# Quartered Grams, moved MLP steps and full-float first lookups in a DLRM tower on one core

## The reference

```
e = stack([tbl_f[ids[:, f]] for f in range(26)], axis=1)      # 2048 x 26 x 128
combined = concatenate([e, dense_x[:, None, :]], axis=1)       # 2048 x 27 x 128
interact = einsum('bfd,bgd->bfg', combined, combined)          # one Gram per sample
z = interact[:, TRIU_I, TRIU_J]                                # 351 pairs
h = concatenate([z, dense_x], axis=1)                          # 2048 x 479
h = maximum(h @ W_top1 + b_top1, 0)                            # 512
h = maximum(h @ W_top2 + b_top2, 0)                            # 256
y = h @ W_top3                                                 # 1
```

## Time and profile before

| | us |
|---|---|
| median of 3 runs | 373.54 (372.81 to 373.73) |
| the profiled execution's own time | 373.32 |
| its span | 371.3 |
| TensorE busy | 340.5 (92%) |
| GpSimd busy (gather issue) | 260.9 (70%) |
| ScalarE busy | 184.3 (50%) |
| VectorE busy | 169.0 (46%) |

### The profile page before, as it was taken

How to read it: one execution, slowest core, us unless ns; L and a number is a source line. 1 busy time by engine, 2 the same in 40 slices (tenths; PEclk the granted TensorE clock), 3 DMA queues, 4 the chain that set the end, 5 groups by cost and what they waited for, 6 DMA issues and landing times.

```text
span 371.3 us, 13577 instructions
## 1 busy us (share of the span) xinstructions
PE 340.5 (92%) x6176; PEld 314.7 (85%) x6176; DVE 169.0 (46%) x380; ACT 184.3 (50%) x233; POOL 260.9 (70%) x265
## 2 busy tenths in 40 slices
PE   0698498889998999999999999999999999999997
PEld 0698497778988988999899998999888989998887
DVE  1999156533533535356244535356244635350220
ACT  3697222583436543473717643473726734375433
POOL 6688777777777777777777777777777777776000
PEclk9999799999998999999999999999999999999999
DMA  7984723212532226221252225321262222222000
GB/s 258 393 307 121 240 60 136 66 51 52 133 128 72 51 51 172 90 69 49 61 201 53 66 52 159 100 67 51 57 209 54 64 53 65 53 56 56 16 4 4
DMA packets 15773, 37.14 MB, mean 100 GB/s; under 512 B 5125, under 2 KB 7813, under 8 KB 15716
## 3 DMA queue, kind: packets, MB, share of 16 engines
q0 software_dynamic: 8192, 16.79, 17.8%
q1 hardware_dynamic: 7524, 19.48, 15.1%
HBM read 36.24 MB, written 0.01 MB: 98 GB/s over the span
## 4 chain that ended last, share of the span: by engine, by line
PE 68%; POOL 20%; issue 7%; DMA 2%; ACT 1%; DVE 1%; SPq 0%; ACTq 0%
PE ps_lk L465 30%; POOL rows L229 20%; PE ps_gram L492 10%; PE ps_tr L477 6%; PE ps_zt L518 6%; PE ps_mlp L518 6%; PE ps_mlp L525 3%; PE ps_zt L525 3%; PE ps_mlp L533 2%; PE ps_lk L546 1%; PE ps_zt L505 1%; DMA ids<-in_ids_onehot 1%; DMA rows<-in_tbl,gather_ids 1%; DVE table L288 1%; PE ps_lk L553 0%
## 5 line engine op out<-in xcount | busy, mean ns | idle before, releaser
L229 POOL DMA_INDIRECT rows<-in_tbl,gather_ids x256 | 259.6, 1014 | 80.5 <-issue 77.1
L465 PE MATMUL ps_lk<-onehot,table 128*128 128x256 f32 x1280 | 167.7, 290 | 14.1 <-DVE onehot L264 13.6
L465 PEld LDWEIGHTS ps_lk<-onehot,table 128*128 128x128 f32 x1280 | 160.4, 197 | 15.3 <-issue 13.9
L264 DVE TENSOR_SCALAR onehot<-ids_from 128x512 fp32r<-128x512 f32 x320 | 125.5, 443 | 92.7 <-PE ps_lk L465 77.0
L332 ACT COPY xt<-ps_tr 128x512 f32<-128x512 f32 x64 | 77.1, 1205 | 93.4 <-PE ps_tr L477 93.4
L492 PEld LDWEIGHTS ps_gram<-xt 128*26 128x26 f32 x4096 | 44.3, 104 | 21.5 <-issue 20.0
L492 PE MATMUL ps_gram<-xt 128*26 128x26 f32 x4096 | 52.6, 193 | 7.6 <-issue 4.3
L322 ACT COPY xt<-ps_lk 128x512 f32<-128x512 f32 x40 | 48.8, 1234 | 17.6 <-PE ps_gram L492 9.0
L272 DVE STREAM_TRANSPOSE zs<-ps_gram 128x832 f32<-128x832 f32 x16 | 16.8, 1050 | 84.2 <-PE ps_gram L492 80.6
L477 PE MATMUL ps_tr<-ident,rows 128*128 128x128 f32 x256 | 39.6, 278 | 6.7 <-DMA rows<-in_tbl,gather_ids 6.1
L477 PEld LDWEIGHTS ps_tr<-ident,rows 128*128 128x128 f32 x256 | 30.1, 141 | 10.0 <-issue 6.4
(11 more groups left out here) (51 smaller groups left out, 128.1 us busy)
## 6 DMA issues: line engine op xcount, KB each, us to landing
ids<-in_ids_onehot SPq DMA_DIRECT2D x8, 768.0 KB
ids<-in_ids_onehot SPq DMA_DIRECT2D x8, 512.0 KB
rows<-in_tbl,gather_ids POOLq DMA_INDIRECT x256, 2.6
w<-in_tbl SPq DMA_DIRECT2D x6, 512.0 KB, 7.5
h<-in_tbl SPq DMA_DIRECT2D x2, 512.0 KB, 5.8
zt<-in_tbl SPq DMA_DIRECT2D x2, 512.0 KB, 6.4
dense_x<-in_dense SPq DMA_DIRECT2D x8, 128.0 KB
zt<-in_dense SPq DMA_DIRECT2D x8, 128.0 KB, 2.9
```

The source lines that it names most:

```text
L229: pool.indirect_dma_start(rows[n % ROW_BUFS][:, r, :], None, t_[f"tbl_{GATHERED[r]}"], bass.IndirectOffsetOnAxis(ap=gather_ids[:, n, r:r + ...
L264: nc.vector.tensor_scalar(onehot[:, u % RING, :, :], ids_from[:, 2 * i:2 * i + 2, :], float(k), None, ALU.is_equal).then_inc(s_unit, 1)
L465: m = nc.tensor.matmul(bank(c, i)[:, j, :], table[:, 2 * i + j, part, k, :], onehot[:, u % RING, j, :], start=(k == 0 and j == 0 and part ...
```

## The change

- **Grams in quarters.** `PARTS` goes from 2 to 4: a Gram call has 32 matmuls. Between two quarters mostly stands an MLP step or a few transposes. The first quarter of tile 0 now stands ahead of `layer1(c-1, 0)` where the half stood behind it, and the first quarter of tile 1 ahead of `layer2(c-1, 0)`.
- **Gathers in eights as before.** A constant `EIGHTS = 2` keeps the half tiles; the Gram counts waited for are doubled, and the start's table `LEAD` is (0, 2, 8, 14, 20) in place of (0, 2, 6, 10, 16).
- **First pair in full floats.** `lookup_first` takes tables 0 and 1 for chunk 0 from their raw buffers, 16 fp32 matmuls in place of 32 fp32r ones, and so needs no high and low parts. These are made last (`SPLIT`), for chunk 1.
- **Start.** The ids of the first two tables are loaded and shifted apart; a tiny activation ahead of them loads ScalarE's table early. Tables from 2 on share three buffers.
- **Order in chunks 0 and 1.** Some transposes and copies stand at other places.

```diff
-PARTS = 2
-LEAD = (0, 2, 6, 10, 16)
+PARTS = 4
+EIGHTS = 2
+LEAD = (0, 2, 8, 14, 20)
+SPLIT = list(range(2, NO)) + [0, 1]
...
-                        pool.wait_ge(s_gpart, max(b - 2 * PARTS, 0) + 1)
+                        pool.wait_ge(s_gpart, (max(b - 2 * EIGHTS, 0) + 1) * (PARTS // EIGHTS))
...
+            def lookup_first():
+                for k in range(KT):
+                    pe.wait_ge(s_unit, k + 1)
+                    for j in range(2):
+                        if k == 0:
+                            pe.wait_ge(s_raw[j], 16)
+                        m = nc.tensor.matmul(bank(0, 0)[:, j, :], raw[j][:, k, :], onehot[:, k, j, :].bitcast(F32),
+                                             start=(k == 0 and j == 0), stop=(k == KT - 1), skip_group_check=True)
+                    if k % USE == USE - 1:
+                        m.then_inc(s_unit_used, 1)
...
             act.wait_ge(s_first, 1)
-            shift_ids(0, 0)
-            for j in range(3):
-                high(j)
+            nc.scalar.activation(warm[:, :], first[:, :], ACT.Identity)
+            shift_first(0, 2, s_ids_a, s_from_a)
+            shift_first(2, CUT[1], s_ids[0], s_from)
+            for n in range(2):
+                high(n)
             shift_ids(0, 1)
...
                 lookup(c, 4)
...
+                gram(c, 0, 0)
                 layer1(c - 1, 0)
-                gram(c, 0, 0)
+                gram(c, 0, 1)
                 if c + 1 < CHUNKS:
                     lookup(c + 1, 0)
                 turn(c, 1, 0)
                 layer1(c - 1, 1)
                 turn(c, 1, 1)
+                gram(c, 0, 2)
                 layer1(c - 1, 2)
-                gram(c, 0, 1)
+                gram(c, 0, 3)
                 turn(c, 1, 2)
                 layer1(c - 1, 3)
                 turn(c, 1, 3)
                 if c + 1 < CHUNKS:
                     lookup(c + 1, 1)
+                gram(c, 1, 0)
                 layer2(c - 1, 0)
-                gram(c, 1, 0)
+                gram(c, 1, 1)
                 if c + 1 < CHUNKS:
                     turn(c + 1, 0, 0)
                     lookup(c + 1, 2)
                     turn(c + 1, 0, 1)
+                gram(c, 1, 2)
                 layer2(c - 1, 1)
                 if c + 1 < CHUNKS:
                     turn(c + 1, 0, 2)
-                gram(c, 1, 1)
+                gram(c, 1, 3)
```

More of the change, by code:

```diff
@@ L104, in build @@
         y = sb("y", [P, TILES])
-        raw = [b[:, a:a + n, :].rearrange("p a s -> p (a s)").rearrange("p (k d) -> p k d", k=KT)
-               for b, a, n in ((h1, 0, T1), (zt, 0, NZ + 1), (w1, 0, 2), (w1, 2, 2), (w2, 0, T1))]
-        RAWS = len(raw)
+        stage = [b[:, a:a + n, :].rearrange("p a s -> p (a s)").rearrange("p (k d) -> p k d", k=KT)
+                 for b, a, n in ((h1, 0, T1), (zt, 0, NZ + 1), (w1, 0, 2), (w1, 2, 2), (w2, 0, T1))]
+        RAWS = len(stage) - 2
+        raw = [stage[j] if j < 2 else stage[2 + (j - 2) % RAWS] for j in range(NO)]
         ps_lk = [pb(f"ps_lk{i}", [P, 2, CS]) for i in range(LB)]
@@ L191, in load_raw @@
             def load_raw(j):
-                if j >= RAWS:
-                    sp.wait_ge(s_low, j - RAWS + 1)
-                sp.dma_start(raw[j % RAWS][:, :, :], t_[f"tbl_{ONE_HOT[j]}"].rearrange("(p k) d -> p k d", k=KT)
+                if j >= 2 + RAWS:
+                    sp.wait_ge(s_low, j - RAWS - 2 + 1)
+                sp.dma_start(raw[j][:, :, :], t_[f"tbl_{ONE_HOT[j]}"].rearrange("(p k) d -> p k d", k=KT)
                              ).then_inc(s_raw[j], 16)
             sp.dma_start(gather_ids[:, :, :], t_["ids_gather"].rearrange("p (t f) -> p t f", t=TILES)).then_inc(s_gids, 16)
-            load_ids(0, 0)
-            for j in range(3):
+            load_first_ids()
+            for j in range(4):
                 load_raw(j)
             load_ids(0, 1)
-            for j in range(3, NO):
+            for j in range(4, NO):
                 load_raw(j)
@@ L285, in _, with low @@
             nc.vector.tensor_copy(first[:, :], first_i[:, :]).then_inc(s_first, 1)
-            for j in range(NO):
-                dve.wait_ge(s_high, j + 1)
-                nc.vector.tensor_tensor(table[:, j, 1, :, :], raw[j % RAWS][:, :, :],
+            def low(n):
+                j = SPLIT[n]
+                dve.wait_ge(s_high, n + 1)
+                nc.vector.tensor_tensor(table[:, j, 1, :, :], raw[j][:, :, :],
                                         table[:, j, 0, :, :].bitcast(F32), ALU.subtract).then_inc(s_low, 1)
-                if j % 2 == 1:
-                    make_units(0, (j - 1) // 2 * KT, (j + 1) // 2 * KT)
+            make_units(0, 0, KT)
+            for i in range(1, LP):
+                low(2 * i - 2)
+                low(2 * i - 1)
+                make_units(0, i * KT, (i + 1) * KT)
+            low(NO - 2)
+            low(NO - 1)
             dve.wait_ge(s_const, 3)
@@ L308, in _, with high, shift_first @@
         def _(act):
-            def high(j):
+            def high(n):
+                j = SPLIT[n]
                 act.wait_ge(s_raw[j], 16)
-                nc.scalar.copy(table[:, j, 0, :, :], raw[j % RAWS][:, :, :]).then_inc(s_high, 1)
+                nc.scalar.copy(table[:, j, 0, :, :], raw[j][:, :, :]).then_inc(s_high, 1)
+            def shift_first(a, b, ready, done):
+                act.wait_ge(ready, 16)
+                nc.scalar.activation(ids_from[:, a:b, :], ids[0][:, a:b, :], ACT.Identity,
+                                     bias=first[:, :]).then_inc(done, 1)
             def shift_ids(c, h):
@@ L566, in _ @@
             pe.wait_ge(s_ident, 2)
-            for i in range(LP):
+            lookup_first()
+            turn(0, 0, 0)
+            for i in range(1, LP):
                 lookup(0, i)
-                turn(0, i // NGR, i % NGR)
+                if i < NGR:
+                    turn(0, 0, i)
             gram(0, 0, 0)
+            gram(0, 0, 1)
             lookup(1, 0)
-            gram(0, 0, 1)
+            gram(0, 0, 2)
+            turn(0, 1, 0)
+            gram(0, 0, 3)
             turn(0, 1, 1)
@@ L577, in _ @@
             turn(0, 1, 3)
-            gram(0, 1, 0)
-            gram(0, 1, 1)
+            for q in range(PARTS):
+                gram(0, 1, q)
             for c in range(1, CHUNKS):
```

41 lines of the change are left out of this document (25 added, 16 removed).

## The result

| | before | changed | 
|---|---|---|
| median, us | 373.18 (4 runs, 372.41 to 373.73) | 383.06 (4 runs, 382.96 to 384.04) |
| the profiled execution, us | 373.32 | 384.04 |
| its span, us | 371.3 | 381.9 |

The ratio is 1.0261, with a 95% interval of 1.0224 to 1.0297: 9.9 us slower. The profiled execution of the changed kernel is the slowest of its four, by 1 us; its span is 10.6 us longer than that of before.

The account below looks back on a forecast made before the run. Gathers were taken to bound the kernel up to 115 us, TensorE after it. Terms -1.65 + 9.4 + 0.8 - 2.0 + 0.5 = +7.05 us on 373.32 gave 380.4, with an 8-in-10 range of 375.5 to 387.

Parts of the forecast that it names:

- The new wait: First quarters behind lookup 4 and the last turn wait for ScalarE's copy: six stalls of 1.35 us and one of 1.3, +9.4.
- The start: Opening: first matmul at 8.8, eight matmuls done by 14.1, ninth gather at 14.65 in place of 16.30 us: -1.65 us.
- the step that earlier gathers give the same time back at the end: Up to 115 us gathers set the time, so starting the ninth 1.65 us earlier was counted in full as -1.65.
- TensorE's arrival: Chunk 2, turn 3: TensorE there at about 110 us, rows at 113.3, so gathers cover changes in its earlier waits.
- Cuts: Gram halves of chunks 2 to 7 cut into quarters: 0.08 us saved for each of 24 halves, -2.0, bounds -6 and +5.
- the quarter itself: A Gram quarter of 32 matmuls was put at 0.55 us plus 0.2 of edge, 0.75 in all.
- The small wait at the chunk's end: Chunk ends 2 to 6: PE reaches turn 3 some 0.15 us before the copy it needs; +0.8, bounds 0 and 2.
- The clock: TensorE's low clock after the row wait near 114 us stays and may last longer: +0.5, bounds 0 and 1.5.
- Rival 1: The new stalls also lower TensorE's clock, near 1.4 us each, six of them 8.4: 388.8 us; chance 0.10.
- Rival 2: Pauses and edges both vanish in Gram quarters, each cut half saving 0.5 us: -2.95, 370.4 us, faster; chance 0.07.
- Rival 3: Pauses come as often per matmul as before and each Gram cut adds 0.2: +4.8 for -2.0, 387.2 us; chance 0.09.
- Rival 4: No difference: pauses gone, edges stay (-6), earlier gathers in full, stalls at lower bound, no clock: +0.75, 374.1 us; chance 0.06.

Follow-up runs that it names:

- e1: The changed kernel with first Gram quarters put back behind layer 1 step 0 in chunks 2 to 7, and behind layer 2 in the last: 372.92 us, ratio 0.9978.
- e2: The kernel before, in halves, with the first half moved ahead of layer 1 in chunks 2 to 7 and ahead of layer 2 in the last: 383.58 us.
- e4: The change's start and order of chunk 0 alone, with Gram halves and the order of the kernel before from chunk 1 on: 374.20 us, ratio 1.0018.
- e7: The kernel before with only LEAD's second number 1 in place of 2, so the ninth gather may start earlier: 373.63 us, ratio 0.9998.
- e5: The changed kernel with turn 3 of tile 2 (chunk 1) behind layer 1 step 0 again, waits of chunks 2 to 7 kept: 382.20 us, ratio 1.025.
- e3: The kernel before with only the second half of each tile cut into quarters, an MLP step between, the first half in one piece: 374.65 us, ratio 1.002.
- e10: The kernel before without the gathers of tiles 6 to 15: 408.43 us on another chip, where before took 489.65, ratio 0.8414.
- e12: The kernel before with LEAD's second number 1 and VectorE's ten low-part subtractions replaced by multiplications by 0: 487.37 us on a chip where before took 489.65.

## Why the prediction was right

380.4 us were forecast with a range of 375.5 to 387, and 383.06 measured: +7.05 forecast, +9.9 found. The large term was right; the small ones were not, and two of their errors nearly cancel.

- **The new wait: right in mechanism, place and nearly in size.** +9.4 forecast, +10.6 by e1 and +9.9 by e2, from seven stalls of 1.26 to 1.30 us in the profile, 8.9 in all. From the start of lookup 4 to that of the Gram 5.33 us pass (209.21 to 214.54), where 3.92 passed to the next operation before: 1.41 a time against the 1.35 forecast. What goes beyond is 0.7 to 1 us that these two runs don't share out cleanly (e1 also takes away cuts, e2 has its pause and clock).
- **The start: the mechanism was wrong.** -1.65 was forecast; e4 measured between -0.1 and +1.5. Three steps failed. The second table landed later than I had read from the rows: the second matmul came at 10.21, where a first one at 8.8 would have let it come at 9.7. The slow first matmuls, put at 3.8 us, lasted some 5.4 in the changed kernel and nearly all of the eight in e4; I had called this a low clock, but the granted clock reads 1.00 over the same stretch of before (12.3 to 16.3), so the name had no row behind it. So the ninth gather gained 0.7 and not 1.65. And the step that earlier gathers give the same time back at the end fails by e7: 1.5 us earlier were used up by longer gathers that begin inside VectorE's subtractions before the 17th had begun. The row for this was in the trace of before, gathers of 1.70 to 1.97 us between 22 and 34 us; I had taken them as the gathers' own.
- **TensorE's arrival: mis-sized.** I had it at its turn 3 of chunk 2 at about 110 and the rows at 113.3. It came at 116.17 and waited for nothing. The adjacent turns and the first quarter of chunk 1 cost waits of 2.1 and 1.6 us, and in this profile the low clock from 78.9 to 85.7; in e1, with the same waits, TensorE was some 2 us earlier at this place. e5 shows how little of that could be had back, since an early TensorE waits for rows and loses clock.
- **Cuts: wrong in sign.** -2.0 forecast for 24 halves. e3 has 12 of them at 0 to +1.6 us. The edges came as I had put them, 0.2 a cut: 0.1 on each side of the new gap. Mis-sized was the quarter itself, 0.55 without its edge: the shortest measured takes 0.65. Where none is left to save, in the last chunk, a cut costs 0.3 us (e3).
- **The small wait at the chunk's end: too large.** 0.8 forecast. In the changed kernel's trace the turn came at 247.39 and the copy that it needs ended at 247.34; at most 0.1 in each of five chunks.
- **The clock: 0.5 forecast, wrong in sign at its place.** The drop at 116 is gone, since no row wait is left there. That gives back some 1.8 us (the chunk from 115.40 took 43.75 us before, the next 41.91). Another drop came in chunk 1. Rival 1, a lower clock in each new stall, is refuted: the chunk from 160 us reads 1.00. But the last chunk of e2 shows that a stall of 1.30 us and a pause behind it can bring it down.
- **Rival 2** (pauses and edges vanish) fails: pauses do get rarer in quarters (the eight of the chunk from 205 us take 6.2 us to their next starts, the four halves of the chunk in the earlier trace rows 6.7), but the edges stay. **Rival 3** is nearest in sign for the cuts, without its size. **Rival 4** is out by the measured time.

By the stages of the profiles the start and chunk 1 cost 1.3 us where -1.65 was forecast, 3 us too low, and the clock at 116 gave back 1.8 where it was to cost 0.5, 2.3 too high. These two nearly cancel, which is luck. All small terms together were forecast at -2.35; e1, which has them but for seven of the cuts, measured -0.8 (-1.6 to 0.0). The right large term carried the result.

## What to carry to other kernels

When an operation is moved ahead of another, ask what that other one covered. Here a step of 1.8 us stood between a producer's last matmul and the consumer of its copy, and moving it cost 1.3 to 1.4 us each time, in full, because TensorE was the bound.

An earlier start of a queue is worth nothing until the stretch behind it has been read: if another engine slows that queue there, the lead is gone before it reaches the bound. And a cut's price is also paid by the neighbours, so sum from start to next start over the whole group.

## What the runs showed of the hardware

- A gather that begins while VectorE subtracts two 128x1024 tensors, and not just at the end of it, ends 0.81 to 0.83 us after the subtraction, and so takes up to 1.97 us instead of 0.95 (before, e7). One that begins just ahead of it isn't held (0.94 us at 22.02 in e10). Of three that begin inside the shorter multiplication of e12 (0.69 us), two end 0.81 and 0.83 us after it, one 1.07.
- Runs of tiny matmuls pause mostly while gathers run: without them 64 take 1.20 us instead of about 1.7, a chunk 40.0 us instead of 42.0 (e10, on another chip than the 42.0). In e12 the half during GpSimd's wait of 7.7 us takes 1.19 us too. A single pause stays without gathers (0.39 us at 393.71 in e10). On that chip the pauses beside gathers were much longer, 1.17 us in e12's rows and 11.6 once, and the same kernel took 489.65 us there and 373.5 elsewhere.
- A matmul step of 256 columns takes 1.74 us between two turns, 1.82 to 1.83 with a Gram on one side, and 1.92 between two Grams (the profiles before and after).
- Behind row waits of 1.20 us (before) and 2.91 us (e5) the granted clock read 0.51 (116 to 119.5 us) and 0.59 (114.4 to 120); there a turn and layer 3 followed the wait. Behind stalls of 1.26 us between lookups and a Gram it stayed at 1.00 (the profile after).
